# Delta rule's last inverse level computed on its 64x64 corner, and five written orders per engine in place of one

## What is computed

```python
xn = layernorm(x)
x  = x + delta_rule_attn(xn) + local_attn_ffn(xn)     # the second: two layers of 8-head window attention and GELU MLP
xn = layernorm(x)
x  = x + latent_attn(xn) + moe(xn)                     # 16 heads of causal attention; 6 experts, top 2, one shared

def delta_rule(q, k, v, beta):                         # 4 heads, dk 128, dv 32
    def step(S, inp):
        q_t, k_t, v_t, b_t = inp
        delta = (v_t - k_t @ S) * b_t
        S = S + outer(k_t, delta)
        return S, q_t @ S
```

## Time and profile before

| | |
|---|---|
| median of 3 runs | 2156.73 us (2155.95 to 2164.53) |
| the profiled execution | 2165.09 us, its span 2163.0 us |
| PE matmul busy | 1882.5 us, 87% of the span |
| DVE, ACT, POOL busy | 1369.2, 943.6, 818.8 us (63, 44, 38%) |
| mean granted clock of PE | 0.93 |
| starts of period 0 to 7 (first `qT` on PE) | 86.6, 305.9, 553, 791, 1031, 1269, 1509, 1747 us |

### The profile page before, as it was taken

One profiled execution on the slowest core, in us unless ns is written; L12 is line 12 of the kernel. 1 busy time (PEld: TensorE's weight loads), 2 busy tenths in 40 slices (PEclk: granted clock), 3 DMA queues, 4 the chain that ended last, 5 costly groups with the idle time before them and its releaser, 6 DMA issues. The chain is left out here.

```text
span 2163.0 us, 40853 instructions
## 1 busy us (share of the span) xinstructions
PE 1882.5 (87%) x15168; PEld 1259.9 (58%) x15168; DVE 1369.2 (63%) x3346; ACT 943.6 (44%) x2449; POOL 818.8 (38%) x819
## 2 busy tenths in 40 slices
PE   2597769999899989998999989898999989987776
PEld 1384438655684658565775568565775568453332
DVE  2354356776768766776768766776668666762441
ACT  1233534366435653365435733465435643453022
POOL 3244634265316533454426522553417432620000
PEclk9699889999999999999999999999999999996575
DMA  4110012200212021201221021201220021200200
GB/s 175 33 44 10 13 29 68 63 16 21 66 38 58 11 62 50 57 10 33 67 59 26 13 67 46 55 15 28 73 61 19 16 57 46 60 4 13 67 1 5
DMA packets 126612, 89.71 MB, mean 41 GB/s; under 512 B 42168, under 2 KB 113976, under 8 KB 126136
## 3 DMA queue, kind: packets, MB, share of 16 engines
q1 hardware_dynamic: 126128, 86.44, 14.9%
q10 hardware_dynamic: 288, 0.67, 0.1%
HBM read 46.84 MB, written 25.17 MB: 33 GB/s over the span
## 5 line engine op out<-in xcount | busy, mean ns | idle before, releaser
L1675 POOL TENSOR_TENSOR soft<-soft,prec 128x512 f32<-128x512 f32 x128 | 133.3, 1044 | 590.3 <-DVE prec L1329 589.7
L1194 ACT ACTIVATE shared<-bank 128x512 f32<-128x512 f32 (+1 forms) x384 | 204.1, 532 | 268.0 <-PE bank L955 267.9
L1483 DVE TENSOR_REDUCE nmx<-bank 128x1 f32<-128x512 f32 (+3 forms) x352 | 224.2, 637 | 86.3 <-PE bank L933 84.7
L1108 ACT ACTIVATE soft<-bank,nmax 128x128 f32<-128x128 f32 x512 | 180.1, 381 | 120.0 <-DVE nmax L1321 119.3
L1636 POOL TENSOR_TENSOR qk_rs<-qk_rs,minus_half 128x16 f32<-128x16 f32 x64 | 188.2, 2940 | 5.3
L633 PE MATMUL bank<-w_sb,hT 128*128 128x512 f32 x256 | 136.2, 627 | 15.6 <-DVE hT L1268 8.0
L955 PE MATMUL bank<-shared 75*128 75x384 bf16 (+3 forms) x512 | 148.7, 316 | 0.0
L954 PE MATMUL bank<-b_sb 128*128 128x128 bf16 x512 | 117.2, 229 | 30.6 <-ACT shared L1194 30.5
L933 PE MATMUL bank<-shared 72*128 72x256 bf16 (+3 forms) x512 | 133.7, 313 | 0.0
L1321 DVE TENSOR_REDUCE nmax<-bank 128x4 f32<-128x512 f32 x128 | 82.4, 685 | 68.6 <-PE bank L690 68.6
L603 PE MATMUL bank<-c_sb,soft 128*128 128x128 f32 x608 | 94.4, 288 | 35.9 <-POOL soft L1675 31.7
(11 more groups left out here) (242 smaller groups left out, 4635.8 us busy)
## 6 DMA issues: line engine op xcount, KB each, us to landing
shared<-parts_dram SPq DMA_DIRECT2D x64, 288.0 KB
vm<-v_f SPq DMA_DIRECT2D x112, 128.0 KB, 2.3
parts_dram<-parts SPq DMA_DIRECT2D x96, 128.0 KB, 2.4
L_dram<-the SPq DMA_DIRECT2D x32, 256.0 KB, 2.3
shared<-X_dram SPq DMA_DIRECT2D x32, 256.0 KB, 2.9
shared<-L_dram SPq DMA_DIRECT2D x32, 256.0 KB, 3.4
w_sb<-weights SPq DMA_DIRECT2D x1, 4167.0 KB, 19.2
x_tm<-x SPq DMA_DIRECT2D x8, 256.0 KB, 3.6
```

Of the source, the lines that this page charges most:

```text
L1108: a = af(v4(p_sb, 2, 4)[:, j, g], place("fS", j)[:, g * P:(g + 1) * P], ACT.Exp, bias=nmax[:, at:at + 1], accum_out=psums[:, at:at + 1])
L1194: af(v4(PTm, 2, GROUP)[:, u % 2, i, 0:n], place("mST")[:, 0:n], ACT.Exp).then_inc(mexp_done, 1)
L1483: reduce(v3(nmx[:], HM)[:, h:h + len(heads), c], v3(place("mS")[:, 0:len(heads) * (c + 1) * P], len(heads)), AX, ALU.max, negate=True).the ...
L1675: tt(p, p, spread(prec[:, at:at + NPAIR], P), ALU.mult).then_inc(fnorm_done, 1)
```

## The change

It does two things.

The first is in `inv_v` and `inv_zx` at k = LEVELS - 1, on PE and DVE. PE multiplies 64 x 64 blocks: weights of 64 rows and 64 columns, 64 moving columns, into the first 64 partitions and the first 64 columns of each head's 128 in the bank (`corner`). The V product reads partitions 64 to 127 of L and Z, the ZV product partitions 0 to 63 of X and Vm. DVE writes 64 x 256 elements of Vm, the corner times -1.0, in place of the masked 128 x 512; and it copies 64 x 256 elements into Z in place of adding 128 x 512. The number of products and of DVE instructions and every semaphore stay as they are.

The second is `ORDER`: five strings per engine, chosen by period: the first for the prologue, then one for period 0, for periods 1 to 6, for period 7 and for period 8. All the strings are new, also the one that the middle periods use.

```diff
 def walk(engine, parts):
     for p in range(-1, BATCH + 1):
         left = {s: collections.deque(x for x in steps if x[0] in parts) for s, steps in period(p).items()}
-        for s in ORDER[engine] if p >= 0 else [s for s in STREAMS for _ in left[s]]:
+        for s in ORDER[engine][0 if p < 0 else 1 if p == 0 else p - BATCH + 4 if p >= BATCH - 1 else 2]:
...
+        def corner(ps):
+            return v3(ps[0:64, 0:2 * P], H0)
...
                         for h in range(H0):
-                            m = mm(ps[:, h * P:(h + 1) * P], Lc[:, h], Zc[:, h], start=True, stop=True)
+                            if k == LEVELS - 1:
+                                m = mm(corner(ps)[:, h], Lc[64:P, h, 0:64], Zc[64:P, h, 64:P], start=True, stop=True)
+                            else:
+                                m = mm(ps[:, h * P:(h + 1) * P], Lc[:, h], Zc[:, h], start=True, stop=True)
...
                     for h in range(H0):
-                        m = mm(ps[:, h * P:(h + 1) * P], Xc[:, h], Vc[:, h], start=True, stop=True)
+                        if k == LEVELS - 1:
+                            m = mm(corner(ps)[:, h], Xc[0:64, h, 0:64], Vc[0:64, h, 64:P], start=True, stop=True)
+                        else:
+                            m = mm(ps[:, h * P:(h + 1) * P], Xc[:, h], Vc[:, h], start=True, stop=True)
...
+                    if k == LEVELS - 1:
+                        ts(v4(Vm, 2, H0)[0:64, c % 2, :, 64:P], corner(place("V", k, c)), -1.0, None, ALU.mult).then_inc(Vm_done, 1)
+                        return
...
+                    if k == LEVELS - 1:
+                        nc.vector.tensor_copy(Zc[0:64, :, 64:P], corner(place("ZV", k, c))).then_inc(Z_done, 1)
+                        return
```

More of the change, by code:

```diff
@@ L48 @@
[L48 to L54 removed]
+        (
+         "fefefffeeeffefeefeeeee"),
+        (
+         "fdddbfddfbfdbbddddfbdbffdddbbddfddbddfdbfdbddddffdbdddbddbdbdbddddbbddbdddedbdddbdddbbbbbbbbdeffefefeffefffbeb"
+         "ebffbbefffbffeebbfebebfebffffbfbbbbffbbbfbbbbbbbbbbbffb"),
@@ new lines @@
+        (
+         "dfddddbmdfmdmdbbdbdfddbdmdfddfmddbmdddffdmbdbddfdbddbddddfmfdmdfbddfdbdeddmddbdbdbdddbdmmdbdbmbmbaambadamabamb"
+         "ababababmbabamfafmfacmcacfcafccmcfacfafcfaccbcfacfambcamcbacbfambaffabacmfcmafcbabcfbaccabfacmacbcafcceafcbaec"
+         "bafcabcaecacbaceacbcaeccafabcfabcebcabafeccbecfecfcecffccbecbbcebbbebcbccbcccccccccccbc"),
+        (
+         "dddddbdmffdddbbdmdbdbddmdfdfddfmfdddbmfdfmbddbmdbdbddmdfmfdfbddfmdddbddbddmdbdddbdmdddbdmmdbdbmbmbamabamdamaba"
+         "mbabamabbabbabmaffmafacmccafcafccmcafcaffacfaccbcfacmfabcmcabcfabmabffabcaffcaabcabcfaccabcabcafcfaccabcfaacab"
+         "cabcabaccbacbcaacabccacbbabccbcccccbcbbccbbbcbccbccccbccccbcccccc"),
@@ new lines @@
+        (
+         "mmmmmmmmmmmmaamamamaamamamamamamaamacmacmacmacmccamcaacacacacaccacmcaaccacaacacaccacacacaccaccacacaccacacacacc"
+         "acacacaccccccccccccccccccccccccc"),),
+    "ACT": (
+        (
+         "effefefeefefeefef"),
+        (
+         "ddfdddfbbdbbdffdfbdfdbddfbfbfdfddbddddbbbddffbdddbbdbdddddbdeffefefeffffbeebffbbfeeffffbebbbffffbfffbbfbbfbfbb"
+         "bfffb"),
+        (
+         "dddddbddfbbdmdfbmfdffbdfddmddmfbbdfbdddmfmddffmdbfbbbddddddbmdbdbbmbmffdcmcfcfcfccfcfcffccbcbcfmcbfbfffcbcfcbb"
+         "mcbfcfcfccbcecbfecfbfcbcecceccbcfbcebfcbecfececfcefccccbcfcccccccfccccb"),
+        (
+         "ddddddbddfbfdbbdmdmddffffbddmfbbmbddmdfdmdfdmfbbbffdbdddddmbddbdbmbmbmfdffccmcfcfccfcfcffccbcfcmcbbbffffcbfccb"
+         "bccbcffcfcccbcfcbbcbcfccbccbbcbcccccccbcccccccccccccbc"),
+        (
+         "mmmmmmmmmmmccmcccccmcccccccccccccccccccccccccccccccccccccccccccccc"),),
@@ new lines @@
+    "DVE": (
+        (
+         "ffffeffeeefefeeeee"),
+        (
+         "bfbddfdbdddbdebbddbdfddddfdeddbbddbddbddddddbdbdbdbdddddddbbddedbbbddbbbbeffeefefbbbffbefbbfbeefebebbbfebfbbbf"
+         "fbbbbbbbbbbb"),
+        (
+         "dbmdbmbfddemddmmdmdfddmbdddmdbdddbmbfdddmddfddbmddemmddbddbmddbdddddmddbdbmbdbmdmmbabeabamabambamaaababbambamf"
+         "amafamfafamaafbabambafamaabmafbmabbafacfaambamababbaaaafaaeaebeaecbababaafabbafebfbebceebbebbbecbc"),
+        (
+         "dbbmbdddfddfmdddmdmmbddmddmdfddbmbbmdmdfddmdbmdmmddbdbddbmdddddddmddbdddmbmbbdmdmmbabambamabambamaaababmbabamf"
+         "amafmaaffaamafababmbafmaaabcafbababafaaaabaaabababaaaambacbababaaabbbbbbcbbbbbcc"),
+        (
+         "mmmmmmmmmmmmmmmmamamamaamamamamamamaamaammamamamaaaamaaaaaaaaacaaaaaaaaaaaaacmaaaaaccc"),),
@@ new lines @@
+    "POOL": (
+        (
+         "fffffeeefeefffff"),
+        (
+         "bfbfffebfbfffffbbbbbdfffffefeebbefffffffefbbffffffbbfffbbffffffbfb"),
+        (
+         "bbfmffbbfeffffffbbbbdbffffffffbbfffffffbbfffffbbebebefeefffbffffbff"),
+        (
+         "bbffmfffbbfffffbbbbdbfffffffffbbffffffbbfffffbbbbbb"),
+        (
+         "m"),),
+    "SP": (
+        (
+         "ffeeefeee"),
+        (
+         "ddedffdffeefeeeffef"),
+        (
+         "deddmfdfmaaffafafafeefeeeec"),
+        (
+         "ddmfddmfaaffaffaac"),
+        (
+         "mmaaaaac"),),
```

9 lines of the change are left out of this document (removed).

## The result

The changed kernel takes 2147.65 us (median of 6 runs, 2141.30 to 2152.89), the kernel before, run beside it, 2162.36 us: ratio 0.9931, 95% interval 0.9912 to 0.9949. I had forecast 2105 us with a range of 2068 to 2138. The direction was right, the size was not. The profiled executions have spans of 2163.0 and 2147.2 us, 15.8 us apart.

The account below looks back on a forecast made before the run. Middle periods were taken as PE-bound, the prologue and periods 0, 7 and 8 as bound by chains of waits. Savings of 14 + 9 + 18 + 7 + 4 = 52 us gave 2113 us profiled, 2105 at the median, range 2068 to 2138.

Parts of the forecast that it names:

- Periods 1 to 6, 18 us in the sum: Middle periods: 1.2 us of PE work and 1.8 us of idle time saved, 3 us per period, 18 in all.
- I take 1.8 us of idle time saved: Middle periods, tail and next start: the new string saves 1.8 of PE's 15.6 idle us per period.
- Rival 2: Middle periods give nothing, idle time only moves; 2134 us in all, chance 0.15.
- These are bound by PE and by little else: Five middle periods: each lasts 238.9 us with 223.2 us of PE work and 15.6 us idle.
- The corner, 1.2 us per period: Last-level V and ZV steps on PE: 0.74 us each instead of 0.89, saving 1.2 us per period.
- Rival 3: Corner does nothing on PE, as shape changes cost what smaller products save; 2115 us, chance 0.10.
- The corner on DVE, counted as nothing: DVE's last-level instructions: eight of 0.42 us instead of 0.69 free 2.1 us per period, counted as no gain.
- The prologue, 10 us: Prologue: k moved ahead of f steps makes the chain to solve 10 us earlier, and this carries through.
- Period 0 (4 us) and period 1 (9 us): Period 0: 2 us at its end and 2 for work leaving; period 1: 9 us from removing PE's wait behind solve.
- Solve's 9.5 us then stand somewhere in period 0's DVE queue, under its 219 us with 111 busy; that is the cover: Period 0 on DVE: solve's 9.5 us moved there were taken as covered by the queue's idle time.
- Periods 7 and 8, 7 and 4 us: Last two periods: own strings with experts earlier, plus the corner, save 7 us (0 to 12) and 4 us.
- Rival 4: Middle periods' tail: solve ahead of x1_apply on DVE adds 9.5 us to each of six; 2180 us, chance 0.05.

Follow-up runs that it names:

- c2_orders_alone: The changed kernel's new orders with whole 128x128 blocks at the last level as before; ratio 1.0029 to the kernel before.
- f1: Changed kernel with unread products filling the tail of periods 1 to 6, fourth gram and solve earlier, final ahead of xn2T; ratio 0.9818 to the kernel before.
- h2: f1 with whole 128x128 blocks at the last level again, on PE and DVE; ratio 0.9916 to the kernel before.
- g1_solve_end_p0: Changed kernel with solve moved behind x1_apply, to the end of DVE's string of period 0; ratio 0.9947 to the kernel before.
- c1_corner_alone: Kernel before with the corner only, walking the old orders in all periods; ratio 0.9994 to the kernel before.

## Why the prediction was wrong

**Periods 1 to 6, 18 us in the sum.** This is the largest miss: periods 2 to 6 gave -1.1 of their 15 us. The step that failed is "I take 1.8 us of idle time saved". It had no row behind it but the gaps themselves. The new middle string by itself made a period 3.3 us longer (238.9 to 242.2 in c2_orders_alone): 1.8 us more idle, which the longer wait for aT behind solve (0.87 to 2.7 us) matches, and 1.6 us more of busy time for the same products, as the time at 1.2 GHz went from 8 to 16 us. The corner then gave 3.1 us back (242.2 to 239.1), so that two misses hid each other. In the changed kernel idle went from 15.6 to 16.3 us per period and the time at 1.2 GHz from 8 to 18 us; the clock was not in the sum at all. Rival 2 (the middle gives nothing) has the right number, and by luck: it had idle time only moving, not one term losing what the other gained.

**What bounds a middle period.** "These are bound by PE and by little else" was half right. Less PE work did shorten a period, by 3.1 to 3.5 us with the new orders. But the tail held some 4 us that no single cure of the clock or of the orders released (239.1, 239.2, 239.4) and both together did (235.0): the handovers with ACT at a granted clock of 0.50, DVE in solve ahead of aT, and x1_apply ahead of xn2T are of nearly one length.

**The corner, 1.2 us per period.** Mis-sized, upwards this time: 2.5 us by the steps themselves and 2.6 by the ratios with the new orders, within the bound of 3.4; with the old order the ratio shows nothing. A lone step costs 0.75 us with its changes of shape, as I had put it (0.74). What the sum left out is that the V and ZV steps use different halves: neighbours overlap and share their changes of shape, and a pair costs 0.90 us, not 1.48. Rival 3 is refuted: the changes cost 0.09 and 0.06 us, no 0.28 is seen at either. The Trainium skill, page "TensorEngine Tiling (Array Packing)", section "Key Properties", states beside the drain that different tiles work in parallel; the alternating rows agree with that, and I had read only the first of the two.

**The corner on DVE, counted as nothing.** With the new orders right: f1 and h2 have the same idle time on PE. In the old order what stood ahead of R in DVE's queue was the gate, and that, not DVE's busy share, decided how much of PE's lead was kept at `seq_u`.

**The prologue, 10 us.** It gave 14.6. I had priced the eight k and f steps at 1.75 to 1.91 us each, 16 us in all. They took 12.2 us, from 35.09 to 47.25, as the granted clock was 1.00 and those from 38.4 us on took 1.02 to 1.12 us each. The fourth reduction ended at 49.1 us, not 52.9. "From 113 to 180 us PE has no gap" is near enough: that stretch of before has two, of 0.8 and 0.7 us.

**Period 0 (4 us) and period 1 (9 us).** Period 0 lost 3.4, period 1 gained 5.1 of its 9 + 3. The step that failed is "Solve's 9.5 us then stand somewhere in period 0's DVE queue, under its 219 us with 111 busy; that is the cover". An average idle share is no cover: solve stood between softmax steps of layer 1's chain, which I had called latency one paragraph before. g1_solve_end_p0 shows 6 us for its place. The gap of 9.93 us is gone, and period 1 still takes 2.9 us more than its successors.

**Periods 7 and 8, 7 and 4 us.** Together they gave 0.6. Period 7 lost 2.5: its new string costs some 4 us against the old one with the corner. That a string of its own would fill its idle time had no row behind it. Period 8's 3.1 us lie within what it varies by itself: 168.0 to 177.6 us with the same instructions. In the rows of before the granted clock of 0.61 stood plainly; I read it as a sign of chains and did not ask what it cost. It cost 12 to 18 us in the changed kernel and 18 with the old string.

**Rival 4** named the right place, solve in front of the tail, and put far too high a price on it. xn2T started 16.6 us behind x1, past my 15, and solve did make aT wait: 0.5 us more than before in the changed kernel, 1.8 more in c2_orders_alone, not the 9.5 of the rival. The opposite order costs 4 us per period.

What stays open: why the chip grants 1.2 GHz in one execution of the same period and not in the next, and so how much of a small difference between two of these kernels is its. Period 0 is the plainest case, 215.7 and 227.9 us with the same instructions. It has 69 us at 1.2 GHz in the changed kernel and 49 in g1_solve_end_p0; a fill there was not tried. Nor was a run made in which the new middle string alone is compared, without the corner, with the string of before behind one and the same period 0; and corner on PE and corner on DVE were never run apart.

## What to carry to other kernels

When a stretch ends in several chains of nearly one length, curing one shows nothing: look in its trace for who waits next, and cure them together before judging any. A queue's idle share over a period is no cover for a 10 us block; the cover is the gap at that place in the queue. And where an engine is at a low granted clock on a chain, work that nobody reads, placed in its waits, can be cheaper than the waits.

## What the runs showed of the hardware

- Products that nobody reads raised the granted clock: 21 bf16 products of 512 columns per period, 4.5 us of work, lifted the stretch from 1240 to 1245 us from 0.50 to 1.00, and with 115 of them period 8 went from 174.1 to 156.1 us.
- The same instructions ran period 8 in 168.0, 170.7, 174.1, 175.5 and 177.6 us, at 117, 133, 140, 141 and 154 us of 1.2 GHz, and period 0 in 215.7 and 227.9 us, at 51 and 81. Single profiles of such a stretch can't be compared below that.
- fp32 products on partitions 0 to 63 and 64 to 127 of neighbouring steps alternate and overlap, across a step's end: 16 of them in 0.90 us, 8 alone in 0.60.
- x1_apply's four TENSOR_SCALAR took 2.57 us beside POOL's TENSOR_TENSOR and 1.10 without. The gate's small TENSOR_SCALAR (128x24) took 0.91 us in c1_corner_alone and 0.50 before, each time ending 0.03 us behind one of POOL's, and 0.18 without. The Trainium skill, page "SBUF — State Buffer", section "SBUF: two separate sides", has DVE and GpSimd share a port pair that, for DVE's instructions in a two-port mode among others, one holds for a whole instruction while the other blocks; the rows agree, as the first two of the four end 0.08 us behind POOL's two (1243.66 and 1244.66) and the other two take 0.33 us each.
